# The last two sparse passes of a graph network: three dense tiles of eight, in groups of four chunks, with the weighted adjacency kept in DRAM between the passes

## The reference, cut to what matters

```python
def gcn_conv(x, src, dst, ew, W, b, n):
    h = x @ W
    ...
    norm = dinv[src] * ew * dinv[dst]
    out = jax.ops.segment_sum(h[src] * norm[:, None], dst, num_segments=n)
    return out + b
z = prelu(gcn_conv(z, src, dst, ew, W0, b0, n), prelu_w)
z = prelu(gcn_conv(z, src, dst, ew, W1, b1, n), prelu_w)
```

## Time and profile before

| | us |
|---|---|
| median of 3 runs (lowest, highest) | 6060.84 (6056.1, 6063.95) |
| the profiled execution | 6057.31 |
| its span | 6055.2 |

### The profile page before, as it was taken

How to read it: one execution, slowest core, us unless ns; L and a number is a source line. 1 busy time by engine, 2 the same in 40 slices (tenths; PEclk the granted TensorE clock), 3 DMA queues, 4 the chain that set the end, 5 groups by cost and what they waited for, 6 DMA issues and landing times.

```text
span 6055.2 us, 91295 instructions
## 1 busy us (share of the span) xinstructions
PE 4082.4 (67%) x23985; PEld 3476.7 (57%) x23985; DVE 2965.7 (49%) x9408; ACT 1617.9 (27%) x3427; POOL 4255.9 (70%) x3756
## 2 busy tenths in 40 slices
PE   4766666666644777777746666666578776677776
PEld 3655555555534777777744444444466665566665
DVE  3544444444416777777751111112454544555455
ACT  3544444444423333333320000000211111111111
POOL 0888888888862777777737777775477774577773
PEclk8888888888877888888866666666699998899997
DMA  6666565565652222222212222221122221222221
GB/s 197 120 112 113 105 112 106 111 113 107 110 81 68 50 50 51 51 50 51 50 43 52 52 52 52 52 52 41 52 53 53 53 53 40 57 53 53 53 53 44
DMA packets 413372, 426.50 MB, mean 70 GB/s; under 512 B 142718, under 2 KB 335846, under 8 KB 413190
## 3 DMA queue, kind: packets, MB, share of 16 engines
q0 software_dynamic: 212992, 247.31, 22.3%
q1 hardware_dynamic: 200198, 177.46, 10.3%
HBM read 337.34 MB, written 87.12 MB: 70 GB/s over the span
## 4 chain that ended last, share of the span: by engine, by line
issue 24%; POOL 23%; PE 21%; DMA 12%; DVE 11%; DVEq 6%; ACT 1%; SPq 1%; POOLq 0%; ACTq 0%
POOL G L594 13%; DMA sums<-G,idx 11%; POOL sums L637 9%; PE psC L1100 7%; PE psA L1027 6%; DVEq L432 4%; PE psC L1037 3%; DVE S L1616 3%; DVE early L1605 2%; PE psE L1090 1%; DVE early L1603 1%; PE psE L1049 1%; PE psD L1042 1%; ACT arena L839 1%; DVE acc L1639 1%
## 5 line engine op out<-in xcount | busy, mean ns | idle before, releaser
L594 POOL DMA_INDIRECT G<-table,idx x1664 | 1690.6, 1016 | 612.8 <-issue 499.2
L637 POOL DMA_INDIRECT sums<-G,idx x832 | 1367.0, 1643 | 345.4 <-issue 211.7
L612 POOL DMA_INDIRECT G<-table,idx x1248 | 1195.1, 958 | 567.9 <-issue 374.5
L950 PE MATMUL psC<-early,S 128*128 128x128 f32 x832 | 199.7, 417 | 505.9 <-ACT G L774 505.9
L950 PEld LDWEIGHTS psC<-early,S 128*128 128x128 f32 x832 | 173.3, 308 | 523.2 <-issue 523.2
L872 ACT COPY arena<-psA 128x600 f32<-128x600 f32 x208 | 136.9, 658 | 1225.2 <-PE psA L1079 1225.2
L1079 PE MATMUL psA<-early 128*128 128x300 f32 x832 | 273.2, 453 | 237.9 <-DVE early L1605 237.9
L1100 PE MATMUL psC<-arena,stage 128*128 128x192 f32 x2548 | 425.3, 329 | 0.0
L1100 PEld LDWEIGHTS psC<-arena,stage 128*128 128x128 f32 x2548 | 420.6, 193 | 1.0 <-DVE acc L1639 0.8
L1639 DVE TENSOR_TENSOR acc<-acc,psC 128x12 f32 x416 | 69.8, 168 | 613.8 <-PE psC L1100 299.9
L1616 DVE TENSOR_SCALAR S<-iota,dloc,ew 128x128 f32<-128x128 f32 x1248 | 350.6, 370 | 30.0 <-DVE dloc L1610 5.5
(11 more groups left out here) (279 smaller groups left out, 9420.6 us busy)
## 6 DMA issues: line engine op xcount, KB each, us to landing
acc<-in_src_row SPq DMA_DIRECT2D x104, 512.0 KB
arena<-in_dst_row SPq DMA_DIRECT2D x104, 512.0 KB
G<-table,idx POOLq DMA_INDIRECT x2912, 2.5
sums<-G,idx POOLq DMA_INDIRECT x832, 3.4
sums<-lohot SPq DMA_DIRECT2D x4, 3200.0 KB, 22.4
table<-stage SPq DMA_DIRECT2D x28, 448.0 KB, 3.0
G<-sums SPq DMA_DIRECT2D x16, 448.0 KB, 5.6
early<-table SPq DMA_DIRECT2D x104, 64.0 KB, 4.7
```

The lines of the kernel that those rows point to most:

```text
L594: pool.indirect_dma_start(G[st.r][:, t * width:(t + 1) * width], None, tables[n], bass.IndirectOffsetOnAxis(ap=idx[st.r][:, t:t + 1], axis ...
L612: pool.indirect_dma_start(G[at.r][:, t * D:(t + 1) * D], None, tables[n], bass.IndirectOffsetOnAxis(ap=idx[at.r][:, t:t + 1], axis=0)).the ...
L637: pool.indirect_dma_start(sums_dram[t % SUMS], bass.IndirectOffsetOnAxis(ap=idx[st.r][:, t:t + 1], axis=0), G[st.r][:, t * D:(t + 1) * D], ...
L950: ins = M.matmul(half_bank[:, at:at + D], S[st.k][:, t * P:(t + 1) * P], h_win[st.r][:, :], start=True, stop=True)
```

## The change

Three tiles of each chunk are dense, five are gathered. The dense sums are formed after 4 chunks (12 tiles, 144 columns) and alternate between two halves of `dense` and between psC and psF. Their adds, three a chunk, stand in the chunks of the following group, in pass 3 each behind the hots of one tile. In pass 3, SP stores every filled `dense` half to DRAM; in pass 4 it loads them, and hots, products and copies are left out. The node numbers are clamped once, and the loads on DVE skip the check of their bounds. Some buffers move into the arena to make room.

```diff
--- before.py
+++ after.py
@@ -41,8 +41,9 @@
-DENSE = 2
-TURN = 8
+DENSE = 3
+GROUP = 4
+TURN = 2 * GROUP
...
+        self.g = k // GROUP
+        self.group = i * 2 + self.g
...
-    NS = TURN * DENSE * SLOTS
+    NS = GROUP * DENSE * SLOTS
+    GROUPS = CHUNKS // GROUP
...
+    adjacency = nc.dram_tensor("adjacency", [GROUPS, P, HIS * NS], F32, kind="Internal").ap()
...
-        dense = arena[:, 0:HIS * NS]
+        dense = [arena[:, behind + 7 * CHUNK - HIS * NS:], arena[:, 0:HIS * NS]]
...
+        adj_moved = [sem(f"adj_moved{g}") for g in range(2)]
...
+        def clamped_node(c, t=0):
+
+            return nc.values_load(dst_i[0:1, bass.ds(c * TILES + t, 1)], engines=(mybir.EngineType.DVE,), min_val=0,
+                                  max_val=N - 1, skip_runtime_bounds_check_because="clamped to 0 .. N - 1 on the chip")
...
+                        if n == 3 and k % GROUP == GROUP - 1 and not (at.first and at.g == 0):
+                            store_adjacency(Spot(i, 0) if at.g else Spot(i - 1, GROUP))
+                        if n == 4 and k % GROUP == 0:
+                            load_adjacency(at)
...
+            def store_adjacency(at):
+
+                sp.wait_ge(mixed["kept"], at.group * (GROUP * DENSE) + GROUP * DENSE)
+                sp.dma_start(adjacency_of(at.group), dense[at.g]).then_inc(adj_moved[at.g], 16)
+
+            def load_adjacency(at):
+
+                if at.first:
+                    sp.wait_ge(begun, 5)
+                    sp.wait_ge(adj_moved[at.g], 16 * (GROUPS // 2))
+                else:
+                    sp.wait_ge(mixed["applied"], at.group + (GROUPS - 1))
+                sp.dma_start(dense[at.g], adjacency_of(at.group)).then_inc(adj_moved[at.g], 16)
...
+                    if n == 3:
+                        store_adjacency(Spot(CHUNKS // TURN - 1, GROUP))
...
+                        if k % GROUP == 0 and not at.first:
+                            act.wait_ge(adj_moved[at.g], i * 16)
                         for t in range(DENSE):
-                            col = (k * DENSE + t) * SLOTS
-                            act.wait_ge(m["counted"], at.c * DENSE + (t + 1 + tiles_before(n)))
-                            A.copy(dense_at(col), counts_in((k * DENSE + t) % 2)).then_inc(m["kept"], 1)
+                            act.wait_ge(m["counted"], at.c * DENSE + (t + 1))
+                            A.copy(dense_at(at.g, k % GROUP * DENSE + t), counts_in((k * DENSE + t) % 2)).then_inc(m["kept"], 1)
...
+                    act.wait_ge(adj_moved[0], 16 * (GROUPS // 2))
...
-            mixed_act(4)
...
-                def dense_sums(i):
-
-                    pe.wait_ge(m["kept"], (i + 1) * (TURN * DENSE) + tiles_before(n))
-                    if not isinstance(i, int):
-                        pe.wait_ge(m["spread"], i * (TURN * DENSE) + (n - 2 + tiles_before(n)))
+                def dense_sums(at):
+
+                    if n == 3:
+                        pe.wait_ge(m["kept"], at.c * DENSE + DENSE)
+                    else:
+                        pe.wait_ge(adj_moved[at.g], at.i * 16 + (GROUPS // 2 + 1) * 16)
+                    if not at.first:
+                        pe.wait_ge(m["spread"], at.group * (GROUP * DENSE) + (n - 2 + spread_before(n) - GROUP * DENSE))
                     for h in range(BLOCKS):
-                        ins = M.matmul(psC[:, 0:NS], stage[:, h * D:(h + 1) * D], dense[:, h * NS:(h + 1) * NS],
-                                       start=(h == 0), stop=(h == BLOCKS - 1))
+                        ins = M.matmul((psC, psF)[at.g][:, 0:NS], stage[:, h * D:(h + 1) * D],
+                                       dense[at.g][:, h * NS:(h + 1) * NS], start=(h == 0), stop=(h == BLOCKS - 1))
                     ins.then_inc(m["applied"], 1)
 
                 def turn(i):
                     for k in range(TURN):
-                        dense_counts(Spot(i, k), k)
-                        gathered_sums(Spot(i, k), k)
-                    dense_sums(i)
+                        at = Spot(i, k)
+                        if n == 3:
+                            dense_counts(at, k)
+                        gathered_sums(at, k)
+                        if k % GROUP == GROUP - 1:
+                            dense_sums(at)
                 return turn
...
-            V.tensor_scalar(dst_i[:, :], dst[:, :], 0.0, None, ALU.max)
+            V.tensor_scalar(dst_i[:, :], dst[:, :], 0.0, float(N - 1), ALU.max, ALU.min)
...
+                def dense_hot(at, k, t):
+
+                    b = (k * DENSE + t) % 2
+                    if not (at.first and k * DENSE + t < 2):
+                        dve.wait_ge(m["counted"], at.c * DENSE + (t - 1))
+                    V.tensor_scalar(lohots[b], iota[:, :], srclo[:, at.column(t)], ew[:, at.column(t)], ALU.is_equal,
+                                    ALU.mult)
+                    V.tensor_scalar(keyhots[b], iotak[:, :], key[:, at.column(t)], None,
+                                    ALU.is_equal).then_inc(m["made"], 1)
...
-                    to = bass.ds(first_node(dve, at.c), P)
+                    to = bass.ds(clamped_node(at.c), P)
...
+                def add_dense(at, k, t, added):
+
+                    to = bass.ds(clamped_node(at.c, t), SLOTS)
+                    if k % GROUP == 0 and t == 0:
+                        dve.wait_ge(m["applied"], at.group + (1 + (n - 3) * GROUPS))
+                    dve.wait_ge(m["spread"], at.c * DENSE + (t + spread_base))
                     dve.wait_ge(s["added"], added)
-                    col = (k * DENSE + t) * SLOTS
-                    V.tensor_tensor(acc[:, bass.ds(node, SLOTS)], acc[:, bass.ds(node, SLOTS)], psC[:, col:col + SLOTS],
+                    col = (k % GROUP * DENSE + t) * SLOTS
+                    V.tensor_tensor(acc[:, to], acc[:, to], (psC, psF)[at.g][:, col:col + SLOTS],
                                     ALU.add).then_inc(m["spread"], 1)
                 def turn(i):
                     for k in range(TURN):
                         at = Spot(i, k)
-                        dense_hots(at, k)
+                        done = Spot(i, k - GROUP) if k >= GROUP else Spot(i - 1, k + GROUP)
+                        for t in range(DENSE):
+                            if n == 3:
+                                dense_hot(at, k, t)
+                            if not (at.first and k < GROUP):
+                                add_dense(done, k, t, at.c - 1)
                         thin_onehot(at, k)
                         if not (at.first and k == 0):
-                            before = Spot(i, k - 1) if k else Spot(i - 1, TURN - 1)
-                            add_gathered(before, None if at.first else (i - 1) * (TURN * DENSE) + k * DENSE)
-                        if not at.first:
-                            for t in range(DENSE):
-                                add_dense(i - 1, k, t, at.c)
+                            add_gathered(Spot(i, k - 1) if k else Spot(i - 1, TURN - 1),
+                                         None if at.first and k < GROUP else at.c * DENSE + (1 - GROUP) * DENSE)
...
-                add_gathered(Spot(end, TURN - 1), end * TURN * DENSE)
-                for k in range(TURN):
+                add_gathered(Spot(end, TURN - 1), (CHUNKS - GROUP) * DENSE)
+                for k in range(GROUP, TURN):
                     for t in range(DENSE):
-                        add_dense(end, k, t, CHUNKS)
-                dve.wait_ge(m["spread"], CHUNKS * DENSE + (n - 2 + tiles_before(n)))
+                        add_dense(Spot(end, k), k, t, CHUNKS)
+                dve.wait_ge(m["spread"], CHUNKS * DENSE + spread_base)
```

More of the change, by code:

```diff
@@ L67, in __init__ @@
         self.r, self.use, self.k = k % ROWS, i * (TURN // ROWS) + k // ROWS, k % 2
-        self.first = isinstance(i, int) and i == 0
+        self.g = k // GROUP
+        self.group = i * 2 + self.g
+        self.i, self.first = i, isinstance(i, int) and i == 0
         self.thin = bass.ds(self.c * TILES + DENSE, TILES - DENSE)
@@ L126, in build_program @@
         acc = sb("acc", max(ACC, 6 * CHUNK))
-        arena = sb("arena", max(ACC, 6 * CHUNK) + 5 * CHUNK)
-        top = arena[:, 0:max(ACC, 6 * CHUNK)]
+        arena = sb("arena", ACC + 7 * CHUNK + TILES * (P + BLOCKS) // 2 + 2 * P)
+        top = arena[:, 0:ACC]
         stage = sb("stage", max(BLOCKS * TW, ACC, 3 * CHUNK))
@@ L141, in build_program @@
         S = [sb(f"S{k}", CHUNK) for k in range(2)]
-        big = [arena[:, max(ACC, 6 * CHUNK) + k * CHUNK:max(ACC, 6 * CHUNK) + (k + 1) * CHUNK] for k in range(5)]
-        dense = arena[:, 0:HIS * NS]
+        rest = arena[:, ACC:ACC + TILES * (P + BLOCKS) // 2 + 2 * P]
+        behind = ACC + TILES * (P + BLOCKS) // 2 + 2 * P
+        big = [arena[:, behind + k * CHUNK:behind + (k + 1) * CHUNK] for k in range(5)]
+        dense = [arena[:, behind + 7 * CHUNK - HIS * NS:], arena[:, 0:HIS * NS]]
+        assert HIS * NS <= behind
```

(27 more changed lines are left out.)

23 lines of the change are left out of this document (8 added, 15 removed).

## The result

The changed kernel takes 6131.3 us (median of 4 runs, 6127.63 to 6140.9) against 6062.4 of the kernel before beside it (6056.1 to 6063.97): ratio 1.0118, interval 1.0101 to 1.0136. Repeated on another chip (after_again, where 6131 was expected), it took 6135.73 against 6053.76 (1.0139, 1.0111 to 1.0166). It is slower, as forecast, but by 69 to 82 us, not by the forecast 152.

What follows compares the result with a forecast made beforehand. POOL was taken to pace both passes, the PE and DVE chain close behind. To the profiled 6057.3 us came +100 (pass 3) and +53 (pass 4): 6210, with 3.5 for the median 6213; forecast 6150 to 6280 (0.54), range 6085 to 6320.

Steps and rivals of the forecast that it cites:

- POOL paces the passes: Passes 3 and 4 of the kernel before: POOL's gathers need 60.3 us a turn, the PE and DVE chain 59.4.
- dense sums and DVE work are in series, twice a turn: Both passes: the first add at a group's head waits for the 12.2 us of matmuls issued just before.
- The add's step of 0.72: DVE: one dense add to the next takes 0.72 us instead of 1.00, without the bounds check.
- the pair of 1.10: DVE in pass 3: a hot and a dense add together cost 1.10 us, the add's load running during the comparison.
- The rival in which POOL stays the pace: Both passes: a group's chain under 25.1 us, each pass losing 131 us, 5796 us in all; chance 0.12.
- the one with dearer terms: Dense sums at 0.1625 a record, unoverlapped hots and adds, or transfers slowing gathers and SBUF reads: 6310 to 6390 us; chance 0.14.
- that in which the load saves nothing: Each group waits for its matrix, above 33 us for 3.69 MB; time above 6250 us; chance 0.02.
- the group of pass 4, 32.9 us: Pass 4: 30.7 us a group plus 1.1 and 1.2 for the clock, rounded down; the pass 878 against 825.1.
- 4.4: DVE in pass 4: a following chunk takes 4.4 us, from adds, dloc, one-hots and a 0.2 margin; three are 13.3.
- the 0.2 which I had added to every chunk: DVE, each chunk: 0.2 us added because the steps summed to 5.75 while measured chunks averaged 5.99.
- the clock stays up: Rival for pass 4: no clock loss, 30.7 us a group, about 6155 us; chance 0.18.
- 35.0 a group: Pass 3: three following chunks, gathered sums 1.5 and dense sums 12.2 in series; the pass 924 against 824.9.

Runs made afterwards that it cites:

- before_adds_first_3: Kernel before, with only DVE's dense adds moved to the head of the chunk, ahead of the hots: 6132.41 us, ratio 1.013.
- split_late_act_2: Changed kernel with dense sums in four parts across the next group's chunks, adds two groups late, adjacency loads issued by ACT: 6059.86 us, ratio 1.0012 to the kernel before.
- sums_last: As split_late_act_2, but on PE the quarter of the dense sums stands ahead of the chunk's gathered sums: 5899.62 us, ratio 0.9745 to the kernel before.
- no_dram: Changed kernel without store and load; pass 4 makes hots, products and copies again: 6222.13 us, ratio 1.0277 to the kernel before.
- warm_p4: Changed kernel; in pass 4 PE also makes two products a chunk from stale hots, which nobody reads: 6084.71 us, ratio 1.0058 to the kernel before.
- late_adds_p4: Changed kernel; in pass 4 alone the dense adds stand behind the one-hots and the gathered add: 6067.08 us, ratio 1.0024 to the kernel before.
- two_dense: Changed kernel with two dense tiles and six gathered ones a chunk: ratio to the kernel before 0.9967 on a faster chip, 1.0193 on a slower one.

## Why the prediction was wrong in size

**What held.** The bound now ("POOL paces the passes") and what decides: "dense sums and DVE work are in series, twice a turn". before_adds_first_3 shows the price of such an order by itself, split_late_act_2 and sums_last that pass 4 falls to POOL's pace once it is gone. The dense sums at 0.1225 us a record are exact: (12.17 - 0.29) / 97, the 0.29 being the length of one record. The add's step of 0.72 measured 0.71 to 0.72, the pair of 1.10 0.97 to 1.08 behind the release and 0.84 behind a gathered add. The stores are free (no_dram), the last adds about 8 us, the first group of pass 4 ended at 48.0 against 47. The rival in which POOL stays the pace fell, the one with dearer terms and that in which the load saves nothing too.

**What failed: the group of pass 4, 32.9 us against 30.77.** 25 x 2.13 = 53 us, the whole of the +53 forecast. Along the rows of one group, from 5656.10 to 5686.46 (30.4 us, 0.4 less than the mean):

| term | forecast | measured |
|---|---|---|
| dense sums, with 1.2 for the clock | 13.4 | 12.9 |
| release to one-hots done | 3.7 | 3.3 |
| three chunks | 13.3 | 11.8 |
| last gathered sums and handover | 2.6 | 2.4 |

(5668.99 - 5656.10; 5672.27 - 5668.99; 5684.03 - 5672.27; the rest.) The largest miss is the chunk, "4.4", which measured 3.92: gathered to dense add 0.61 instead of 0.74, dense add to dloc 0.19 instead of 0.27, the one-hots 1.29 to 1.38 instead of 1.42, and the 0.2 which I had added to every chunk because measured chunks of before averaged 5.99 against a sum of 5.75 was not there. I carried a surplus over without knowing its cause. In the six chunks of the earlier trace rows no hot waits for a product; half of the 1.4 us are two second dense adds that came 0.35 late, with nothing named (1.20 and 1.17 us idle where the earlier trace rows have 0.83). The first of them, in the kernel before:

```profile
5449.34 0.17 DVE L1639 TENSOR_TENSOR acc<-acc,psC 128x12 f32 x1 [1.20 <-issue]
```

A gathered add came 0.4 late in the same way. In the group of the changed kernel above, the steps have no such delay. What causes it stays open.

**The clock.** It fell as forecast (0.74), and the last gathered sums cost the 1.1 forecast (2.50 against 1.35). The dense sums lost 0.6, not 1.2 (12.63 on average against 12.02). By warm_p4 the whole price is 43 us, less than the 55 that I had put on it. The Trainium skill, "TensorE: Matmul & The Clock Gate", section "HAM oscillation — how this bites in real kernels", has each burst after a wait start throttled. The trace agrees on the sign (2.50 instead of 1.35 us). The rival "the clock stays up" had a time nearer to the result, 6155, by luck: the clock did fall.

**Pass 3**, 34.12 against 35.0 a group, +76 against +100, is the same fault in small, and in time another 24 us: 12.0 for 12.2, 4.15 for 4.5 (5088.27 to 5092.42), 16.5 for 16.8, 1.36 for 1.5. Each term was rounded to the dear side, 22 us in 25 groups. The third hot's wait of 0.55 to 0.79 a chunk for a product was not in my sum at all; the margin of 0.2 and the dear pair covered for it, which was luck. A slip of the sum in the rival "POOL stays the pace" changed nothing: its lower ends give 49 + 25 x 30.6 = 814 us and 55 + 25 x 28.1 = 758, not both 760 to 790; the time, 5979, is in the 5960 to 6020 that it named.

## What to carry to other kernels

When a reader of a long result is moved to right behind its issue, the result's whole length becomes serial, even if it is double-buffered: a second buffer helps only if the reader asks one group late. Taking work from the busiest engine gains until the next ring closes, so find that ring (here third hot, product, sums, one-hots, or, in late_adds_p4, dense sums, adjacency load, indices, gathers) before you count the gain. A margin whose cause was not found is no property of another step; look for its rows before you carry it over.

## What was not expected of the hardware

More work made pass 4 shorter: two useless products a chunk gave back 43 us through the clock (warm_p4), which rose from 0.74 to 0.98. And the kernel before took some 6050 us on three chips and 7160 on two others, with pauses of PE for which the profile names nothing. On these even the sign of two_dense turned (0.9967 against 1.0193).
